# A graph layer on Trainium2: more blocks computed without gathers, layer 4 turned round, segments spread between f32 matmuls

## The reference

```
h   = max(layernorm(x), 0)
agg = segment_sum(h[src], dst) / max(degree, 1)
g   = relu(agg @ Wg + h @ Ws + bg)          # layer 1, 128 -> 128
g   = tanh(g @ W1 + b1)                     # layer 2, 128 -> 512
g   = tanh(g @ W2 + b2)                     # layer 3, 512 -> 512
out = x + g @ W3 + b3                       # layer 4, 512 -> 128
```

## Time and profile before

| | |
|---|---|
| median of 3 runs | 2306.32 us (2306.32 to 2311.11) |
| profiled execution | 2319.8 us |
| its span, first to last instruction | 2317.8 us |
| mean granted TensorE clock | 0.805 of full speed |
| busy: TensorE, weight loads, VectorE, ScalarE, GpSimd | 63%, 47%, 47%, 22%, 45% |

### The profile page before, as it was taken

The page is one execution under the profiler, slowest core; times in us unless marked ns, Lnnn a source line. Parts: engine busy times, 40 slices in busy tenths (PEclk is TensorE's granted clock), DMA queues, the critical chain, the costliest instruction groups (busy, mean ns, idle before and its releaser), DMA issues.

```text
span 2317.8 us, 26082 instructions
## 1 busy us (share of the span) xinstructions
PE 1469.9 (63%) x8355; PEld 1078.8 (47%) x8355; DVE 1094.6 (47%) x3610; ACT 513.0 (22%) x1064; POOL 1040.5 (45%) x1107
## 2 busy tenths in 40 slices
PE   0021756477676766767676776768675776767679
PEld 0011634345454554545454553546454553645457
DVE  2461854545372644645372644546362643645331
ACT  1341212113030311213030312213030311213032
POOL 7346045543546254443446264543446254443530
PEclk9955967777787787988787887878787777878789
DMA  6221012121212012121212112121212012121210
GB/s 217 77 99 45 13 32 80 41 65 35 78 35 83 24 51 71 44 71 39 73 36 84 28 51 65 46 71 39 70 37 83 23 53 67 43 71 37 76 34 12
DMA packets 87991, 133.17 MB, mean 57 GB/s; under 512 B 24631, under 2 KB 66238, under 8 KB 84414
## 3 DMA queue, kind: packets, MB, share of 16 engines
q0 software_dynamic: 35072, 71.90, 11.6%
q1 hardware_dynamic: 48572, 58.03, 7.7%
q10 hardware_dynamic: 4226, 1.63, 0.3%
HBM read 118.49 MB, written 12.99 MB: 57 GB/s over the span
## 4 chain that ended last, share of the span: by engine, by line
PE 57%; issue 23%; another core or an unknown queue 10%; DVE 5%; ACT 4%; DMA 0%; DVEq 0%; SPq 0%; ACTq 0%
PE banks L816 16%; PE banks L782 10%; PE banks L693 8%; PE banks L767 8%; PE banks L829 5%; PE banks L801 3%; ACT arena L1101 2%; PE banks L790 1%; DVE arena L1199 1%; PE banks L793 1%; PE banks L740 1%; PE banks L825 1%; ACT dense L1079 1%; DVE arena L1203 1%
## 5 line engine op out<-in xcount | busy, mean ns | idle before, releaser
L606 POOL DMA_INDIRECT ring<-h_table,idx_slot x1032 | 978.2, 948 | 1194.3 <-DVE idx_slot L1421 826.8
L816 PE MATMUL banks<-dense,w 128*128 128x256 f32 (+1 forms) x1568 | 436.4, 428 | 120.5 <-issue 85.2
L816 PEld LDWEIGHTS banks<-dense,w 128*128 128x128 f32 x1568 | 319.7, 215 | 190.0 <-issue 98.4
L767 PE MATMUL banks<-xin,arena 128*128 128x256 f16 (+1 forms) x1470 | 238.3, 304 | 188.7 <-issue 112.9
L782 PE MATMUL banks<-arena 128*128 128x257 f16 x1470 | 227.6, 304 | 142.2 <-issue 140.7
L767 PEld LDWEIGHTS banks<-xin,arena 128*128 128x128 f16 (+1 forms) x1470 | 146.3, 107 | 278.4 <-issue 146.0
L693 PE MATMUL banks<-ring,onehot 128*128 x1197 | 215.8, 301 | 79.2 <-issue 63.2
L1101 ACT CAST arena<-banks 128x512 f16<-128x512 f32 (+1 forms) x375 | 206.9, 579 | 252.3 <-PE banks L767 122.0
L1517 DVE TENSOR_SCALAR arena<-node,qd 128x256 f16<-128x256 f16 x735 | 151.1, 284 | 229.9 <-remote 178.3
L782 PEld LDWEIGHTS banks<-arena 128*128 128x128 f16 x1470 | 150.9, 105 | 218.2 <-issue 190.0
L1351 DVE TENSOR_SCALAR onehot<-iota,rel 128x128 f16<-128x128 f16 x1220 | 209.9, 279 | 2.3
(11 more groups left out here) (145 smaller groups left out, 1193.2 us busy)
## 6 DMA issues: line engine op xcount, KB each, us to landing
arena<-unit_codes SPq DMA_DIRECT2D x15, 1568.0 KB
ring<-h_table,idx_slot POOLq DMA_INDIRECT x1032
xin<-in_x_dram SPq DMA_DIRECT2D x6, 1024.0 KB, 5.5
h_table<-xin SPq DMA_DIRECT2D x6, 1024.0 KB, 3.8
tblk<-h_table SPq DMA_DIRECT2D x48, 128.0 KB
xblk<-in_x_dram SPq DMA_DIRECT2D x48, 128.0 KB
out_dram<-dense SPq DMA_DIRECT2D x48, 128.0 KB
arena<-in_x_dram,arena POOLq DMA_INDIRECT x64
```

The source lines that it names most:

```text
L606: nc.gpsimd.indirect_dma_start(out=ring_tiles[:, k * GT + j, 0:2 * D], out_offset=None, in_=table, in_offset=bass.IndirectOffsetOnAxis(ap= ...
L767: mm = nc.tensor.matmul(to, wide_l[0:rows, piece % WSLOTS, k, j, :], tab[0:rows, 2 * g + j, :], start=(j == 0), stop=(j == 1))
L816: mm = nc.tensor.matmul(l3_ps[c][:, 0:w], w2[:, q, c * P:(c + 1) * P], h2T[:, q, 0:w], start=(q == 0), stop=(q == HC - 1))
```

## The change

- `PB` goes from 34 to 32, so that 17 blocks are units and 32 pool blocks remain. A period has four steps or two (`PERIOD_STEPS`, eleven and six of them); one with two steps has one pool block and the unit. The loops that counted bodies are replaced by a list `PERIODS` and an order of blocks `ORDER` that all engines share; a block's slot is its place modulo 3.
- Segments are no longer one piece behind another: `begin_sums` waits and reads the window's start, and `sum_tiles` issues single tiles. The first segment of a period runs two tiles at a time between the f32 matmuls of layer 3, the second and third beside layer 4 and layer 2 (`layers_and_segment`), the fourth beside layer 3. The unit's pairs are spread one or two to each f32 matmul of layer 3, not three to each half.
- Layer 4 holds w3 stationary, streams h3T (256 columns), and gives the result with features on partitions (`outT_ps`). ScalarE adds b3 while it copies it to SBUF (`take_out`), and TensorE turns it back with two transposes (`turn_out`). `split_b3` and the bf16 rows go.
- The 19 comparisons of a step's one-hots become one instruction with two broadcast operands, one of them in PSUM.
- On VectorE the first step of a period moves behind three pieces of `match_codes`. The turning of a period's first block moves in front of the last two pieces of the sums before.

```diff
-PB = 34
+PB = 32
+PERIOD_STEPS = (4, 4, 2, 4, 4, 2, 4, 2, 4, 4, 2, 4, 2, 4, 2, 4, 4)
-PAIRS_BETWEEN = (3, 3, 3, 3, 3, 3, 2, 2)
+PAIRS_BETWEEN = (1, 1, 2, 1, 1, 2, 1, 2, 1, 1, 2, 1, 1, 2, 1, 2)
...
+        outT_ps = banks[:, 4, 0:BLK]
...
+            def begin_sums(s):
                 pe.wait_ge(mean_done, s)
+                for g in (2 * s + 1, 2 * s + 2):
+                    pe.wait_ge(gathered[g % RG], 16 * GT * (g // RG))
                 pe.wait_ge(onehot_ready, s - 2)
+                return pe.value_load(lead_row[0:1, s:s + 1], min_val=0, max_val=REACH)
+
+            def sum_tiles(s, lead, tiles):
+                for j in tiles:
+                    mm = nc.tensor.matmul(main_ps[:, 0:2 * D + 1], onehot[:, s % 2, j, :],
+                                          ring_column(window_slot(s, lead, j)), start=(j == 0), stop=(j == W - 1))
+                    if j == W - 1:
+                        mm.then_inc(seg_done, 1)
...
+            def layer4(k, beside=None):
+                for q in range(HC):
+                    if q in (0, HC - 1):
+                        pe.wait_ge(h3_ready, HC * k + (HC if q else HC - 1))
+                    mm = nc.tensor.matmul(outT_ps, w3[:, q], h3T[:, q], start=(q == 0), stop=(q == HC - 1))
+                    if q == HC - 1:
+                        mm.then_inc(outT_done, 1)
+                    if beside:
+                        beside(q)
+
+            def turn_out(k, carried=0):
+                pe.wait_ge(outT_ready, k + 1)
                 at(pe, oblk_ready, k)
+                at(pe, carry_taken, carried)
+                for t in range(NT):
+                    mm = nc.tensor.transpose(out_ps[:, t], outT[:, t * P:(t + 1) * P], ident[:])
+                mm.then_inc(l4_done, 1)
...
+            def layers_and_segment(k, following, step, carried=0):
+                lead = begin_sums(step)
+                layer4(k, lambda q: sum_tiles(step, lead, [q]))
+                sum_tiles(step, lead, range(HC, 12))
+                turn_out(k, carried)
+                layer2(following, k + 1, lambda c: sum_tiles(step, lead, range(12 + 2 * c, min(14 + 2 * c, W))))
...
+                def beside_first(slot):
+                    sum_tiles(steps[0], lead, range(min(2 * slot, W), min(2 * slot + 2, W)))
+                    if slot == 9 and not last:
                         carry_groups(n + 1)
+                    if slot == HC * HC - 1 and n:
+                        turn(k + 1)
+                    pr = 3 + sum(PAIRS_BETWEEN[:slot])
+                    gather_pairs(n, range(pr, pr + PAIRS_BETWEEN[slot]))
...
                 turn_codes(n + 1)
-                sum_unit(n, range(NP))
+                sum_unit(n, range(NP - 2))
+                turn(PLACE[PERIODS[n + 1][1][0]])
+                sum_unit(n, range(NP - 2, NP))
...
+            def take_out(k):
+                act.wait_ge(outT_done, k + 1)
+                at(act, l4_done, k)
+                nc.scalar.activation(outT[:], outT_ps, ACT.Identity, bias=b3c[:, 0:1]).then_inc(outT_ready, 1)
...
-                for j in range(n):
-                    ins = nc.vector.tensor_scalar(onehot[:, b, j], iota16[:], rel[:, b, j:j + 1], None, ALU.is_equal)
-                ins.then_inc(onehot_ready, 1)
+                nc.vector.tensor_tensor(onehot[:, b, 0:n], iota16[:].unsqueeze(1).to_broadcast([P, n, P]),
+                                        held.unsqueeze(2).to_broadcast([P, n, P]), ALU.is_equal
+                                        ).then_inc(onehot_ready, 1)
...
+            def period(n):
+                if not last:
+                    place_edges(n + 1)
                 match_codes(n, [4])
+                if not last:
+                    count_groups(n + 1)
+                match_codes(n, [5, 6])
+                step(steps[0])
+                match_codes(n, [7])
+                if not last:
+                    take_carry(n + 1)
+                    load_edges(n + 1)
+                    scan_places(n + 1)
                 match_nodes(n, [0, 1])
+                residual(k)
+                step(steps[1])
                 match_nodes(n, [2, 3])
```

More of the change, by code:

```diff
@@ L619, in _ @@
                     gather_pair(i * (RG // 2) + k // 2, k)
+            for pair in range(GROUPS // RG * (RG // 2), GROUPS // 2):
+                gather_pair(pair, 2 * pair % RG)
             wait_alone(pool, idx_ready, GROUPS // 2 - RAWG // 2 + 1, issuing)
@@ L871, in gather_beside @@
                 gather_pairs(n, range(2))
[L872 removed]
+                layer2(first, k)
                 gather_pairs(n, range(2, 3))
[L874 to L877 removed]
+                lead = begin_sums(steps[0])
+                def beside_first(slot):
+                    sum_tiles(steps[0], lead, range(min(2 * slot, W), min(2 * slot + 2, W)))
+                    if slot == 9 and not last:
@@ new lines, in period @@
+                if n:
+                    unit = blocks[1]
+                    after_layer1(unit, k + 1)
+                    take_out(k)
+                    after_layer2(unit, k + 1)
+                    after_layer3(unit, k + 1, range(HC - 1))
+                    if third is not None:
+                        take_rows(PLACE[third])
+                    after_layer3(unit, k + 1, [HC - 1])
+                else:
+                    take_out(k)
+                    take_rows(PLACE[third])
@@ new lines, in period @@
+            def period(n):
+                steps, blocks = PERIODS[n]
+                last = n == UNITS - 1
+                k = PLACE[blocks[0]]
+                if not last:
+                    place_edges(n + 1)
+                match_codes(n, [4])
+                if not last:
[7 more added lines that the diff above has]
+                    scan_places(n + 1)
```

492 lines of the change are left out of this document (225 added, 267 removed).

## The result

The changed kernel takes 2315.1 us (median of 13 runs, 2308.8 to 2322.2) and the kernel before 2307.4 us (13 runs); the ratio is 1.0029, interval 1.0019 to 1.0039. So it is slower by 0.3%, where 2253 us were forecast. The profiled execution has a span of 2318.0 us.

The account below looks back on a forecast made before the run. TensorE's order of work, slowed during gathers, was taken to set the end. The middle of -24 and -66, -45, with -8 for prologue and tail gave -53 against 2306.3: 2253 us, range 2170 to 2315.

Parts of the forecast that it names:

- the price of a full period: Period of four steps, by instruction prices: 130.5 - 3.0 - 2.7 + 2.0 - 1.5 = 125.3 us.
- chained gathers: Rival: a period's fourth gather follows the third without a gap, 9.1 us lost each time; 2353 in all full periods; chance 0.13.
- two sums: Ten full and six short periods against 1827 us: by matmul counts 1803 (-24), by instruction prices 1761 (-66); middle taken, -45.
- The other parts of the kernel: Prologue and tail: no wait before layer 3, cheaper layer 4s outside periods, some interleaving in the last period; together -8 us.
- The stretches of 23 us: Periods cut where GpSimd begins and ends its 16 gathers; TensorE slowed there, 12 to 13 us lost per step.
- The swap of units: 17 units and 32 pool blocks: at the old kernel's prices 2 x 130.5 - 6 x 41.6 = +11 us.
- Layer 4's hop: Rival: the extra ScalarE pass and its hand-offs are uncovered, 0.8 us each, 49 times, 39 us back, 2292; chance 0.12.
- the term of -3.0 us a period: Layer 4 with fewer matmul instructions: 0.41 us less where TensorE runs free, 1.3 in a gather, two of three there.
- Spread segments: Tiles between f32 matmuls: -2.7 us a period, +2.0 for the lost cover before the first pair, -1.5 for pairs' waits.
- One-hots: One instruction for 19 on VectorE: 2.85 us against 3.23, on the path once a period at most; counted as nothing.
- Hand-offs covered: Rival: interleaved tiles bring all gather stretches to 82 matmuls, 84 us more saved, 2169; chance 0.17.
- The gathers are not the cause: Rival: gathers don't slow TensorE, so dropping 4 stretches saves nothing, 50 us back, 2303; chance 0.08.

## Why the prediction was wrong

That TensorE's progress in and between the gathers sets the end was right for this kind of chip, and so was the price of a full period: the windows give 125.3 to 126.5 us for those that the sum describes (125.3 forecast). The price is luck, as told below. The step that failed is the one on chained gathers: "the segment ends the slow stretch, so a short gap should stay", with a chance of 0.13. The segment doesn't end with the slow stretch. Behind the first full period TensorE completed it 8.9 or 9.0 us into the third gather in seven of eight and 10.4 in one, and the gap stays only where the signal of its end is held until the gather is over. In five of nine the signal got through, and the fourth gather followed the third by 0.30 us. The price, 9.1 us, was nearly right: those five took 136.2 us on average, 10.9 more than the forecast, 55 us together, so that five were enough where the prediction worked out six. The order of periods alone brings 50 of them back (2316 to 2266), and whole segments 40: two quite different edits that both end the chain.

The prediction took the middle of its two sums, 126.0 us for a full period and 87.0 for a short one. Against this the five chained ones lost 51 us, the first one 8 and the six short ones 4. With some 126 us for the tenth full period, whose gathers stand as in those without a chain, all sixteen took 1845 us, 18 more than before, and the forecast had 45 less. The other parts of the kernel gave 17 us and not 8, and the span came out as before (2318.0 against 2317.8).

One reading was off as well. The stretches of 23 us are not cut where GpSimd ends its 16 gathers: in the one that ends at 1226.9 us its last instruction ends at 1223.7. They end where TensorE's signals came again, some 3 us later.

- *The short periods* took 87.6 us, between the two sums (84.7 and 89.2).
- *The swap of units* was forecast to cost 11 us and costs 16 where no fourth gather is chained. Right, and mis-sized by 5.
- *The first full period* takes 134.5 us, but it took 133.5 before as well. One gather is chained there in both kernels; that of the kernel before is the one of the earlier trace rows.
- *Layer 4's hop*, forecast at 0.8 us each if uncovered, shows 5.0 us each (247.5 over 49). The idle time isn't the price, though: without it the kernel is 4 to 6 us faster, not 247. And the term of -3.0 us a period isn't there: with layer 4 as before the full periods without a chain take 124.2 to 126.3 us, with the turning back 125.3 to 127.3 in the two traces.
- *Spread segments*, -2.7, +2.0 and -1.5, come to nothing in a period without a chain (124.9 to 125.4 whole, 125.3 to 127.3 spread), and the spreading brings the segment's end early enough for the chains: together 40 us slower. The wait ahead of the first pair came as said (50.5 us over 17, 3.0 each, 2.0 forecast).
- *One-hots*, counted as nothing. The duration was read about right (2.69 against 2.85 us, where the 19 took 3.23), the effect was not: one instruction is worth 44 us in this kernel. The Trainium skill (VectorE: DVE Perf Modes, "The perf-mode tier table" and the cycle table of the errata section) lets the 19 small ones be the faster form, an estimate of 1.8 us by its cycles; the runs here disagree, in their duration (3.23 us) and in the kernel's time. The errata section itself says that this row comes out too low for a single operation and gives a measured fixed term of about 150 cycles in place of 58, by which the 19 would be an estimate of 3.6 us; the trace lies nearer to that.
- *Hand-offs covered* (2169) didn't come. *The gathers are not the cause*: by it the swap of units would have cost 11 + 50 = 61 us on kind A, and it costs 16, so four gather stretches less are worth about what was forecast. On kind B TensorE isn't held up beside gathers, 477 matmuls in four of them, and the Trainium skill's rule (SBUF — State Buffer, "SBUF: two separate sides") agrees with that trace. On kind A the run with half of the rows doesn't speak against the rule either: halving the data left the stalls.

The full period came out as forecast although layer 4 and the spread tiles gave nothing: two terms of -3.0 and -2.2 us were wrong, and something not counted stands in their place, which is luck. The one-hots are the only part shown to move a period without a chain by as much (7 us, in the changed kernel's order); they were counted as nothing because VectorE was taken to be off the path. How much of the 56 us of the 15-unit form is theirs and how much the new order's stays open: the run that was to show it, the kernel before with the one-hots alone, fell on kind B twice. Open too is what the chips of kind A have that holds TensorE's signals back, whether GpSimd's issuing is what does it, and why a gather with a late second instruction lets a signal through for longer.

Three versions beat both kernels on kind A: 15 units (2250), the reordered periods (2266), whole segments (2276). On kind B only the kernel before with the one-hots in one instruction is measurably faster than the kernel before, by 0.2 to 0.3%; the 15-unit form is the only one run on both kinds that is clearly ahead on one and not clearly behind on the other.

## What to carry to other kernels

Where one engine's work holds up another's signals, price a hand-off by where it falls in that work: it costs nothing in the free part of the stretch and up to all the rest of it in the held one, so the idle time in front of a wait doesn't tell what removing it brings. Something that is finished earlier can also start its successor earlier: ask of every segment moved forward what its end releases, when the engine that waits for it really learns of it, and whether a gap that let others through is lost. Where a loop on one engine has one odd turn, look at which piece of the other engines' work meets it. And time both kernels on more than one chip before a choice like the number of units rests on a price: here it was worth 16 us on one kind and 96 on the other.

## What the runs showed of the hardware

- Two kinds of chips for one program: 2307 against 1451 us, with gather instructions of the same length (957 and 958 ns).
- On the slower kind no compute engine ran an instruction for 21.8 us of a gather that followed another directly, though no semaphore in the profile explains it.
- There a segment that TensorE completed 8.9 us into a gather was known to VectorE only at 22.6 to 22.8 us, when the gather was over. In gathers whose second instruction came some 2.1 us behind the first, and not 1.25, it was known at 10.6 to 16.3 us if complete by 9.1, and never before 23.3 if complete at 11.5 or later.
- Half of the rows in an indirect gather shorten its instruction by 5% (957 to 912 ns) and the stalls not at all.
- 19 comparisons of 128x128 in separate instructions took 3.23 us and one of 2432 elements 2.69; the 0.54 us a step were worth 44 us in this kernel on the slower kind, though VectorE is idle half of the time.
